# Sixteen state slots and seven decay buffers in place of fourteen and nine, in four conditioned layers with two state-space scans

## What is computed

```python
def step(h, inp):
    dt_t, B_t, C_t, u_t = inp
    dA = jnp.exp(dt_t[:, :, None] * A)
    h = h * dA + (dt_t * u_t)[:, :, None] * B_t[:, None, :]
    y = jnp.einsum('bdn,bn->bd', h, C_t)
    return (h, y)
...
y = jnp.transpose(ys, (1, 0, 2)) + u * D_param
y = y * jax.nn.silu(z)
return jnp.einsum('bsd,ed->bse', y, out_proj_w)
```

## Time and profile before

| | us |
|---|---|
| median of 3 runs | 1989.25 (1987.35 to 1989.5) |
| the profiled execution, its own time | 1993.09 |
| its span, first to last instruction | 1991.0 |
| first unit scan starts | 114.4 |
| last side scan starts | 1925.3 |
| busy PE, DVE, ACT, POOL | 1802.9, 1808.0, 1705.0, 1760.8 |
| DVE's unit scans, spread and beside | 594 x 1.21, 430 x 1.20 |
| POOL's weightings and injections | 510 x 2.37, 215 x 2.37 |
| granted clock of PE, mean | 0.97 |

### The profile page before, as it was taken

How to read it: one execution, slowest core, us unless ns; L and a number is a source line. 1 busy time by engine, 2 the same in 40 slices (tenths; PEclk the granted TensorE clock), 3 DMA queues, 4 the chain that set the end, 5 groups by cost and what they waited for, 6 DMA issues and landing times. The chain is left out here.

```text
span 1991.0 us, 29259 instructions
## 1 busy us (share of the span) xinstructions
PE 1802.9 (91%) x9252; PEld 1254.3 (63%) x9252; DVE 1808.0 (91%) x2019; ACT 1705.0 (86%) x3226; POOL 1760.8 (88%) x766
## 2 busy tenths in 40 slices
PE   8969589999989999998999999999999999697878
PEld 7545455757667575756767575766757575555666
DVE  6459899999999999999999999999999999999983
ACT  3388688999989999999989999999989998878652
POOL 0059999999999999999999999999999999999960
PEclk9889699999999999999999999999999999898999
DMA  7035555454545545454545645455545555555430
GB/s 283 1 105 159 166 169 159 143 169 149 171 136 174 169 153 173 141 169 150 155 145 160 183 149 170 145 178 160 160 145 157 161 163 170 150 163 159 148 101 11
DMA packets 163784, 302.29 MB, mean 152 GB/s; under 512 B 18904, under 2 KB 27312, under 8 KB 162096
## 3 DMA queue, kind: packets, MB, share of 16 engines
q1 hardware_dynamic: 153110, 287.45, 47.6%
q10 hardware_dynamic: 10522, 12.99, 2.0%
HBM read 292.98 MB, written 5.29 MB: 150 GB/s over the span
## 5 line engine op out<-in xcount | busy, mean ns | idle before, releaser
L965 POOL TENSOR_TENSOR state<-state,c_rows 128x1024 f32<-128x1024 f32 x510 | 1194.4, 2366 | 35.0 <-DVE state L1593 20.7
L1593 DVE TENSOR_TENSOR_SCAN state<-decay,mix_banks 128x512 f32<-128x512 f32 x594 | 693.6, 1206 | 14.4 <-ACT decay L1299 1.0
L2028 PE MATMUL bank<-const_sb,state 128*128 128x128 f32 x4096 | 539.2, 280 | 42.9 <-POOL state L965 42.1
L2028 PEld LDWEIGHTS bank<-const_sb,state 128*128 128x128 f32 x4096 | 478.7, 144 | 154.0 <-issue 76.0
L1590 DVE TENSOR_TENSOR_SCAN state<-mix_banks,state 128x512 f32<-128x512 f32 x430 | 503.7, 1203 | 27.2 <-ACT mix_banks L1280 24.1
L956 POOL TENSOR_TENSOR state<-kept,b_rows 128x1024 f32<-128x1024 f32 x215 | 508.0, 2366 | 18.0 <-PE bank L2028 13.8
L1299 ACT ACTIVATE decay<-kept,ssm_pack 128x512 f32<-128x512 f32 x594 | 405.2, 715 | 5.0 <-issue 2.6
L1583 DVE TENSOR_TENSOR mix_banks<-kept,mix_banks 128x1024 f32<-128x1024 f32 x297 | 364.4, 1227 | 25.2 <-ACT mix_banks L1288 16.1
L1280 ACT ACTIVATE mix_banks<-kept,ssm_pack 128x512 f32<-128x512 f32 x430 | 289.4, 681 | 39.9 <-DVE state L1593 27.6
L1848 PE MATMUL bank<-kept,conv_diag 128*128 128x512 f32 x496 | 224.6, 594 | 2.7 <-ACT kept L1220 2.3
L983 ACT ACT_TABLE_LOAD x158 | 202.7, 1283 | 20.8 <-DVE prep_minus L1419 11.6
(11 more groups left out here) (206 smaller groups left out, 2207.9 us busy)
## 6 DMA issues: line engine op xcount, KB each, us to landing
b_rows<-flat_rows SPq DMA_DIRECT2D x512, 256.0 KB, 3.7
c_rows<-flat_rows SPq DMA_DIRECT2D x512, 256.0 KB, 3.7
conv_diag<-conv_diag SPq DMA_DIRECT2D x8, 1024.0 KB, 7.4
out<-x_res ACTq DMA_DIRECT2D x8, 512.0 KB, 3.6
ssm_pack<-ssm_pack SPq DMA_DIRECT2D x2, 1907.0 KB, 12.1
x_next<-x ACTq DMA_DIRECT2D x6, 512.0 KB, 6.0
x_again<-x_dbl ACTq DMA_DIRECT2D x16, 128.0 KB, 2.8
state<-ada_w SPq DMA_DIRECT2D x1, 1536.0 KB, 14.4
```

Of the source, the lines that this page charges most:

```text
L965: pool.tensor_tensor(st, st, by_pair(c_rows[:, row % ROWS]), ALU.mult).then_inc(m_prod, 1)
L1593: ins = dve.tensor_tensor_scan(st, decay[:, nth(g) % DECAYS], mixed, 0.0, ALU.mult, ALU.add)
L2028: ins = pe.matmul(y_banks[c2][:, t * P:(t + 1) * P], state[:, g % STATES, t * P:(t + 1) * P], ident, start=False, stop=(g == BANK_SUMS[g / ...
```

## The change

Two state slots more and two decay buffers fewer; both are rows of 128x512 float32, so the SBUF in use is the same, 23 rows. No function is changed. The order tables are all replaced by new ones: of `STEPS`, 167 of 430 bank decays, 96 of 297 B rows, 230 of 594 side decays, 105 of 215 injections, 193 of 510 weightings and 433 of 1,024 sums get another number, most of them by one to three quarters. They cluster in passes 1 to 3, 5, and 9 to 12. The order in which units are summed is the same, and so is the kind of every pair. The count of ACT's table loads goes from 158 to 160.

```diff
-BANKS, DECAYS, STATES, ROWS = 3, 9, 14, 4
+BANKS, DECAYS, STATES, ROWS = 3, 7, 16, 4
...
-FIRST_BASES = {'att': (-55, -28), 'setup': -50, 'prep': -28}
+FIRST_BASES = {'att': (-53, -27), 'setup': -49, 'prep': -27}
...
-ATT_BASES, LATE_BASES = (13, 99, 152, 218), (33, 194)
+ATT_BASES, LATE_BASES = (12, 99, 152, 218), (33, 194)
```

Of the tables two lines stand for all, the first of the bank decays:

```diff
-    "bank": (4, 2, 5, 1, 13, 2, 8, 7, 8, 8, 8, 3, 8, 6, 7, 5, 12, 8, 12, 2, 2, 5, 7, 4, 11, 8, 8, 8, 15, 5, 6, 8,
+    "bank": (2, 4, 7, 0, 12, 2, 8, 6, 8, 3, 8, 3, 6, 8, 8, 4, 10, 5, 12, 1, 6, 7, 8, 6, 10, 8, 8, 8, 15, 5, 12, 8,
```

More of the change, by code:

```diff
@@ L214 @@
         255, 258),
-    7: (199, 199, 201, 202, 202, 201, 203, 202, 202, 202, 204, 211, 213, 214, 220, 222, 227, 235, 237, 239, 249,
-        253, 256),
-    8: (183, 183, 186, 190, 192, 197, 197, 198, 198, 198, 198, 199, 199, 200, 203, 208, 216, 218, 218, 218, 218,
+    7: (198, 198, 200, 200, 201, 200, 203, 202, 202, 202, 203, 203, 207, 209, 214, 220, 222, 227, 232, 238, 242,
+        248, 250),
+    8: (187, 187, 190, 191, 191, 196, 198, 198, 198, 198, 199, 199, 200, 201, 206, 212, 216, 218, 218, 218, 218,
@@ L225 @@
-    12: (186, 186, 190, 198, 200, 200, 201, 201, 201, 201, 202, 201, 203, 203, 207, 213, 219, 222, 222, 222, 222,
+    10: (194, 194, 198, 199, 199, 200, 202, 201, 201, 201, 203, 202, 206, 218, 221, 227, 233, 237, 239, 244, 251,
+         253, 256),
+    11: (198, 198, 200, 200, 200, 201, 202, 202, 202, 202, 203, 207, 209, 211, 217, 221, 224, 229, 236, 237, 240,
+         248, 250),
+    12: (186, 186, 190, 198, 199, 200, 201, 200, 200, 200, 202, 201, 203, 203, 207, 213, 219, 222, 222, 222, 222,
@@ L226 @@
          222, 222),
-    13: (187, 187, 194, 197, 200, 202, 202, 203, 203, 203, 204, 204, 206, 209, 215, 220, 221, 224, 224, 224, 224,
+    13: (187, 187, 194, 196, 197, 201, 202, 203, 203, 203, 204, 204, 206, 209, 215, 220, 221, 224, 224, 224, 224,
          224, 224),
-    14: (183, 183, 198, 198, 199, 202, 204, 208, 208, 208, 210, 209, 211, 213, 217, 220, 227, 233, 236, 239, 244,
-         250, 254),
-    15: (0, 0, 26, 74, 82, 75, 89, 110, 121, 190, 191, 191, 192, 194, 197, 197, 201, 198, 201, 205, 208, 208, 209),
+    14: (183, 183, 198, 198, 199, 202, 204, 208, 208, 208, 210, 209, 211, 213, 217, 220, 227, 230, 236, 238, 243,
+         249, 254),
@@ L232 @@
+    15: (0, 0, 2, 74, 82, 75, 89, 110, 123, 190, 191, 191, 192, 194, 197, 197, 201, 198, 201, 205, 208, 208, 209),
 })
 TAIL_STAGES = by_name(TAIL_NAMES, {
-    0: (97, 98, 98, 99, 100),
-    1: (1, 55, 60, 63, 66),
+    0: (91, 99, 99, 99, 100),
+    1: (1, 54, 60, 63, 66),
     2: (44, 58, 62, 68, 70),
     3: (50, 53, 60, 69, 79),
-    4: (55, 71, 76, 77, 80),
+    4: (55, 74, 77, 77, 79),
     5: (57, 61, 64, 68, 76),
-    6: (54, 60, 63, 64, 73),
+    6: (54, 60, 63, 67, 71),
     7: (46, 63, 67, 69, 78),
-    8: (64, 74, 77, 77, 80),
@@ L243 @@
-    9: (57, 61, 62, 63, 72),
-    10: (60, 63, 64, 71, 77),
-    11: (58, 61, 65, 74, 78),
-    12: (58, 75, 77, 77, 80),
-    13: (45, 61, 63, 74, 79),
-    14: (53, 62, 66, 71, 80),
-    15: (45, 59, 62, 74, 80),
+    8: (62, 71, 76, 77, 79),
+    9: (57, 61, 64, 68, 72),
+    10: (57, 61, 62, 63, 73),
+    11: (57, 62, 66, 74, 78),
+    12: (60, 76, 77, 78, 80),
+    13: (45, 61, 63, 74, 78),
+    14: (46, 62, 67, 75, 79),
+    15: (44, 59, 62, 74, 80),
 })
-SETUP_STAGES = dict(zip(SETUP_NAMES, (0, 22, 24, 50, 58, 63, 61, 67, 83, 86, 71, 96, 139, 168), strict=True))
+SETUP_STAGES = dict(zip(SETUP_NAMES, (2, 23, 26, 51, 59, 65, 63, 69, 85, 88, 72, 98, 137, 170), strict=True))
@@ L255 @@
 STEPS = {
-    "bank": (4, 2, 5, 1, 13, 2, 8, 7, 8, 8, 8, 3, 8, 6, 7, 5, 12, 8, 12, 2, 2, 5, 7, 4, 11, 8, 8, 8, 15, 5, 6, 8,
[13 rows of a table removed]
-    "row": (5, 5, 12, 3, 5, 6, 10, 8, 8, 12, 5, 8, 10, 5, 8, 4, 9, 7, 8, 2, 8, 8, 8, 8, 5, 8, 8, 8, 6, 7, 7, 12, 4,
[9 rows of a table removed]
-    "beside": (13, 8, 17, 20, 22, 21, 32, 30, 37, 5, 5, 8, 11, 12, 15, 17, 28, 27, 29, 33, 27, 31, 19, 22, 25, 24,
[22 rows of a table removed]
-    "inject": (17, 25, 31, 24, 23, 15, 25, 22, 20, 19, 24, 20, 12, 24, 32, 26, 21, 21, 11, 15, 14, 20, 18, 23, 17,
[8 rows of a table removed]
-    "weight": (12, 7, 8, 8, 5, 8, 6, 8, 6, 8, 8, 9, 6, 15, 13, 10, 15, 10, 6, 10, 6, 12, 8, 12, 20, 18, 17, 13, 17,
[18 rows of a table removed]
-    "sum": (37, 34, 31, 27, 23, 21, 19, 16, 14, 11, 13, 9, 11, 10, 19, 31, 28, 34, 31, 28, 24, 21, 18, 15, 11, 9,
[11 rows of a table removed]
+    "bank": (2, 4, 7, 0, 12, 2, 8, 6, 8, 3, 8, 3, 6, 8, 8, 4, 10, 5, 12, 1, 6, 7, 8, 6, 10, 8, 8, 8, 15, 5, 12, 8,
[13 rows of a table added]
+    "row": (9, 9, 13, 5, 5, 5, 9, 8, 5, 10, 5, 8, 11, 4, 7, 4, 9, 8, 8, 3, 8, 8, 8, 8, 5, 8, 10, 8, 6, 8, 7, 12, 5,
[9 rows of a table added]
+    "beside": (7, 3, 13, 15, 18, 19, 30, 33, 45, 5, 4, 7, 10, 12, 15, 17, 27, 18, 20, 22, 28, 31, 19, 22, 25, 29,
[22 rows of a table added]
+    "inject": (11, 30, 31, 23, 23, 18, 25, 14, 24, 26, 21, 25, 8, 21, 28, 21, 25, 18, 14, 19, 15, 21, 18, 17, 23,
[8 rows of a table added]
+    "weight": (5, 6, 8, 8, 5, 9, 6, 8, 6, 8, 8, 9, 9, 15, 13, 10, 10, 7, 13, 10, 11, 11, 7, 18, 17, 17, 16, 13, 12,
[18 rows of a table added]
+    "sum": (37, 34, 30, 27, 23, 20, 18, 16, 13, 11, 13, 10, 13, 11, 14, 26, 24, 21, 32, 29, 25, 22, 19, 15, 25, 23,
[11 rows of a table added]
             15, 22, 19, 16, 25, 24, 22, 19, 37, 34, 30, 29, 26, 25, 22, 19, 17, 15, 26, 23, 23, 23, 27, 25, 22, 20,
             19, 21, 18, 14, 15, 12, 18, 22, 37, 33, 30, 26, 23, 20, 37, 35, 31, 28, 26, 23, 21, 18, 24, 21, 31, 27,
[1 row of a table removed]
[1 row of a table added]
             26, 23, 20, 19, 16, 14, 24, 20, 17, 14, 10, 7, 23, 20, 17, 24, 22, 18, 30, 26, 29, 26, 29, 25, 22, 18,
```

22 lines of the change are left out of this document (9 added, 13 removed), and 368 rows, old and new, of tables (ATT_STAGES, PREP_STAGES, STEPS).

## The result

| | median, us | range, us | runs |
|---|---|---|---|
| kernel before | 1989.5 | 1986.92 to 1995.47 | 7 |
| changed kernel | 1993.76 | 1992.75 to 1995.49 | 7 |

The ratio is 1.0022, with a 95% interval of 1.0012 to 1.0031. The changed kernel is slower by 4.3 us, where I forecast 1.7 us less and called it no change. The time lies in my range, the sign is wrong.

The account below looks back on a forecast made before the run. The ring DVE - PSUM bank - ACT was taken to set the pace, with POOL nearly full. Terms -0.5 + 1 - 1.2 - 1 + 0 + 0 = -1.7 us gave 1991.4 profiled, 1987.5 as a median; range 1977.5 to 1996.

Parts of the forecast that it names:

- no change: Whole kernel: the forecast that the time stays within 0.2% of before, 4 us; chance 0.50.
- Step 1: Two more state slots: POOL's 13.8 us of waits for TensorE's sums mostly go; -0.5 us, ends 0 and -13.8.
- Step 2: Two fewer decay buffers: eleven side decays on ACT could wait for scans; +1 us, ends 0 and +9.8.
- Step 3: ACT at unit 767: bank decay now ahead of two skip scalings, DVE's 1.53 us wait goes; gain 1.2 us.
- Step 4: DVE's waits for bank decays: eleven stay, 15.8 us, with unit 49's 3.82 us still there; rest -1, ends -6.8 and +6.8.
- Step 5: Opening: first scan about 1 us earlier, nothing left by unit 10; net 0, ends -1.35 and +0.6.
- Step 6: ACT's table loads: 160 instead of 158, both new ones in the last pass; 0, ends 0 and +2.6.
- A: Rival: POOL is the bound, so its saved waits come back, 10.7 us, giving 1978.5; chance 0.12.
- B: Rival: the new tables win 4.5 of step 4's open 6.8 us, giving about 1983; chance 0.21.
- C: Rival: late decay buffers hold ACT, delaying bank decays and DVE; 9.8 us plus 1 for loads, 1997.4; chance 0.17.

Follow-up runs that it names:

- e1: Kernel before with its old order tables, but sixteen state slots and seven decay buffers: ratio 1.0001 to the kernel before.
- e4: The changed kernel measured again without edit: ratio 1.0033 to the kernel before, 1996.42 us.
- e5: Kernel before with sixteen slots and seven buffers, plus the new tables in the opening and first pass alone: ratio 1.0027 to the kernel before.
- e3: The kernel before measured again without edit: ratio 1.0002.
- e6: The changed kernel with the old tables in the opening and first pass: ratio 0.9997 to the kernel before.
- e14: Kernel before with one swap on ACT: bank decay of unit 40 ahead of the SiLU of u and z; ratio 1.0010.
- e11: The changed kernel with the old numbers of units 16 to 63 and the old second preparation: ratio 0.9999 to the kernel before.
- e7: Kernel before with sixteen slots and seven buffers, plus the new tables in passes 9 to 12 alone: ratio 1.0063 to the kernel before.

## Why the prediction was wrong

**Step 1, the slots: right in what they are worth, not in where the waits go.** The injections' waits on sums fell from 13.8 to 2.0 us (I said about 3), and by e1 this is worth nothing; I took 0.5. But I had POOL's waits for DVE rise by most of it. They rose by 4.9 us in e1 and not at all in the changed kernel, where 9.0 us came back as waits of weightings and dt*u for sums. The longest two of the eight waits were not the one at 794.37 but those at 208.71 and 257.84, 2.66 and 2.82 us.

**Step 2, the decay buffers: right in kind.** Side decays wait 7.3 us for scans in the changed kernel, nine times, under the 10 that I named as the limit, and 5.1 us in e1, where I had counted 6.5. Of these, e1 passes nothing on. I took 1 us.

**Step 3, unit 767: the mechanism right, the gain smaller.** The wait of 1.53 us is gone, but the B row behind the scalings is now 1.01 us late. I had looked at what stands ahead of the one late instruction, and not at the next one behind those that it overtook. Of the 1.53 us of wait some 0.5 is saved at this place, where I took 1.2.

**Step 4, what is not re-ordered: here it failed.** I sorted DVE's old waits by whether the instructions right ahead of them had moved, called eleven of them unchanged at a price of 0, and took -1 for the rest with 6.8 us either way. I priced no place where a bank decay came in time before. The loss comes from such a place, unit 41, and from one of the eleven, unit 49. Units 32 to 64 take 58.8 to 59.4 us in the changed kernel, e4 and e5, and 55.2 to 55.7 in e3, e1 and e6: 3.1 to 4.2 us more, inside the ends that I gave, on the other side. 1.3 to 1.6 us of it is the idle time of DVE up to unit 41, by e14 the swap's own. The rest stands at unit 49. The wait of 3.82 us there, which I took for a property of the order, was one of that execution: e3 has 1.84 us, e1 2.26 and e6 0.20, with the same order in this pass. The copy that it hangs on takes 7.8 us in before, and 6.4, 6.2 and 5.1 us in these three. The changed kernel and e4 have 4.03 and 4.11. So "still there", my sign for step 4, came true by luck. The price of the swap could have been read from the trace of before. Unit 37 is scanned until some 189 us there, so a bank decay of unit 40 put in front waits until then, and the SiLU, which ran at 188.60, goes behind it, with both table loads.

**Step 5, the opening: right as far as can be seen.** The first product no longer waits for the B row but for POOL (11.3 us, one time). The first scan about 1 us earlier, which I named as a sign, isn't in this pair of profiles (114.8 us, 114.4 in before). It shows only on average over all of them (see e11), and by unit 16 nothing is left of it.

**Step 6, table loads: as forecast.** 160 of 1,283 ns, as counted, and by e6 nothing that they cost.

**The rivals.** A (POOL the bound) and B (the tables win more) fall with e1 and e6. C had the right sign and the right ring (an instruction on ACT whose buffer is not yet free, bank decays behind it, DVE waiting), but the wrong buffer: it is a PSUM bank and not one of the seven decay buffers. I had priced only the buffer whose number changed, though the tables moved the decays of both kinds. I was too sure of "no change": 0.17 for slower was low for a change that rewrites 1,224 numbers, when I had looked mainly at places that already showed a wait. And the top of the range, 1996, is not where three quarters of C's 9.8 us have passed on but 86% of them, 8.45 us above 1987.55.

**What stays open.** By medians the changed kernel loses 4.3 us and, in e4, 6.1 (1996.42 against 1990.3), and the places found make 3.1 to 4.2 of it. The rest is not located. The first profile of before doesn't fit the comparison: there units 32 to 64 take 58.3 us, nearly as long as in the changed kernel, 2.0 of the 2.6 us over e3 by its 3.82 us at unit 49. I compare with four other profiles of the old first pass (e1, e3, e6, e7), which agree within 0.5 us, and with e11. The trace of e14 has 58.4 us, with the same slow stretch behind as before (last section), and so shows the swap at its place only. The stretches from unit 80 on differ by up to 6 us between two profiles of one kernel (1657.6 and 1663.2 in the changed kernel, 1660.5 and 1665.0 in before), so single profiles can't find it, and e11, which exchanges only units 16 to 63, is free of the whole loss within 0.12%. No version beat the kernel before.

## What to carry to other kernels

On an engine that works in order, look at every instruction that moved ahead of a long block (a table load, a large activation, a DMA issue), and find in the old trace when its buffer comes free. If that is later than the block was ready, the block pays the difference, and so does all behind it, even where the old trace shows no wait of these instructions. A second cause can hide behind the first. The changed kernel has the ratio 1.0022 and 1.0033, with PE's order undone 1.0027, with ACT's 1.0019, with both 1.0012; in units 32 to 64 it is 58.8 to 59.4 us, then 57.7, 57.3 and 55.8. And take a second profile before arguing on a wait behind a DMA: here one copy took 5.1 to 7.8 us in kernels of one order.
